# First stage of a two-layer kernel: GpSimd makes both halves of twelve weight splits, two tables move to VectorE

## The reference, cut to what matters

```
# layer 1
c  = x @ W_base^T + b_base + 2 * sum_e w[e] * (x @ As[e]^T) @ Bs[e]^T   # lora with per-row weights
xn = (c - mean) * rsqrt(var + 1e-5) * gamma + beta
s  = max|xn| / 127 ;  q = round(xn / s) ;  wq = alpha * ternary(weight)
x  = x + (q * s) @ wq^T
# layer 2
routing: softmax of 8 logits per row, the best 2 experts, their weights normalised
out = sum over the 2 experts of w * mlp_expert(x) + mlp_shared(x)     # mlp: gelu(x G) * (x U), then D
x = x + quantised_ffn(out)                                            # int16 activations, 4-bit weights
```

## Time and profile before

| | us |
|---|---|
| median of 3 runs (398.55 to 400.49) | 399.46 |
| the profiled execution | 398.53 |
| its span in the profile | 396.8 |
| busy TensorE | 347.6 |
| busy VectorE | 332.6 |
| busy ScalarE | 263.1 |
| busy GpSimd | 231.7 |

### The profile page before, as it was taken

The page is one execution under the profiler, slowest core; times in us unless marked ns, Lnnn a source line. Parts: engine busy times, 40 slices in busy tenths (PEclk is TensorE's granted clock), DMA queues, the critical chain, the costliest instruction groups (busy, mean ns, idle before and its releaser), DMA issues.

```text
span 396.8 us, 6241 instructions
## 1 busy us (share of the span) xinstructions
PE 347.6 (88%) x1759; PEld 286.6 (72%) x1759; DVE 332.6 (84%) x700; ACT 263.1 (66%) x340; POOL 231.7 (58%) x404
## 2 busy tenths in 40 slices
PE   7899987999999999999999999899999972035997
PEld 6677665768898989989898977688577651023797
DVE  4589558976999999999999988876679899989894
ACT  3656687857566665666656545455477899999650
POOL 2647875997466473847465016822095567993552
PEclk9989989999999999999999999999999997555999
DMA  5998994845352443535332005100000000000022
GB/s 165 341 408 295 347 307 133 304 159 213 111 208 108 157 164 113 205 108 186 134 121 91 3 2 170 42 2 0 1 2 1 1 0 0 0 2 1 0 108 106
DMA packets 19850, 47.77 MB, mean 120 GB/s; under 512 B 2787, under 2 KB 8934, under 8 KB 17254
## 3 DMA queue, kind: packets, MB, share of 16 engines
q1 hardware_dynamic: 18342, 47.16, 34.0%
q10 hardware_dynamic: 1472, 0.20, 0.3%
HBM read 33.10 MB, written 12.58 MB: 115 GB/s over the span
## 4 chain that ended last, share of the span: by engine, by line
PE 56%; ACT 12%; DVE 11%; POOL 9%; issue 6%; DMA 4%; POOLq 1%; ACTq 0%; DVEq 0%
PE ps L384 55%; ACT tS L1308 3%; ACT UA L1308 3%; ACT ps L1308 2%; ACT U L1308 2%; DMA wscr<-wst 2%; POOL WD L1547 2%; POOL XCh L1544 2%; DVE unread L1265 2%; DVE O_i L761 2%; DMA bsr<-in_L_cond_Bs_dram 1%; DVE Hl L755 1%; PE ps L381 1%; POOL Hl L1547 1%; POOL wst L1547 1%
## 5 line engine op out<-in xcount | busy, mean ns | idle before, releaser
L1628 POOL CAST xg<-XT 128x64 fp32r x264 | 81.2, 354 | 52.6 <-DVE Hl L755 25.4
L384 PE MATMUL ps<-xg,Wr 128*128 128x384 f32 (+1 forms) x480 | 98.6, 353 | 1.1 <-POOL xg L1628 0.8
L384 PEld LDWEIGHTS ps<-xg,Wr 128*128 128x128 f32 x480 | 85.8, 188 | 8.2 <-POOL xg L1628 1.1
L1308 ACT ACTIVATE Hh<-HbS 128x512 fp32r<-128x512 f32 (+2 forms) x72 | 56.5, 785 | 47.6 <-DVE HbS L755 47.5
L755 DVE TENSOR_TENSOR HbS<-Gb,ps 128x512 f32<-128x512 f32 (+2 forms) x72 | 63.2, 878 | 21.3 <-PE ps L384 18.3
L1308 ACT ACTIVATE Gb<-ps 128x512 f32<-128x512 f32 (+2 forms) x72 | 54.0, 750 | 30.5 <-PE ps L384 28.8
L755 DVE TENSOR_TENSOR Hl<-HbS,Hh 128x768 fp32r<-128x768 f32 (+2 forms) x57 | 59.4, 1042 | 3.5 <-ACT Hh L1308 3.0
L761 DVE SCALAR_TENSOR_TENSOR C<-ps,Wt,C 128x32 f32 x264 | 52.4, 277 | 2.9 <-PE ps L384 2.6
L384 PE MATMUL ps<-XT,SHh 128*128 128x512 f32 x128 | 45.7, 399 | 0.8 <-DVE XT L755 0.4
L1547 POOL TENSOR_TENSOR Hl<-HbS,Hh 128x512 fp32r<-128x512 f32 x15 | 19.5, 1297 | 38.5 <-ACT Hh L1308 38.3
L1308 ACT ACTIVATE ps<-G,S 128x1024 int32<-128x1024 f32 (+2 forms) x30 | 35.8, 1250 | 6.2 <-DVE O_i L761 5.6
(11 more groups left out here) (223 smaller groups left out, 710.8 us busy)
## 6 DMA issues: line engine op xcount, KB each, us to landing
Wr<-wscr SPq DMA_DIRECT2D x20, 1024.0 KB, 4.8
wscr<-wst SPq DMA_DIRECT2D x16, 512.0 KB, 5.9
stg<-n_L_cond_skill_gate_dram SPq DMA_DIRECT2D x8, 256.0 KB, 7.0
stg<-in_L_cond_skill_up_dram SPq DMA_DIRECT2D x8, 256.0 KB, 7.4
wdr<-n_L_cond_skill_down_dram SPq DMA_DIRECT2D x8, 256.0 KB, 5.8
xscr<-X SPq DMA_DIRECT2D x8, 256.0 KB, 6.0
X<-xscr SPq DMA_DIRECT2D x8, 256.0 KB, 4.3
out_dram<-X SPq DMA_DIRECT2D x7, 256.0 KB, 2.0
```

The source lines that it names most:

```text
L384: return e.matmul(o_, l, r, start=start, stop=stop, skip_group_check=True)
L1308: return e.activation(o_, i_, func, **kw)
L1628: last = e.tensor_copy(xg[:, i % XR, :, T * s:T * s + T].rearrange("p a t -> p a t"), XT[:, :, :, bass.ds(regs[s - a_], 1)].rearrange("p a ...
```

## The change

It has six parts.

1. `SPLITS` is now (0, 2, 2, 1, 2, 1, 2, 1, 1, 2, 3, 2). The first `NP` = 12 splits, those of rounds 1 to 8, are made wholly on GpSimd: a copy into the high part (`k_whi`), then the low part. The waits for the load and for the store of the ring's place go with them from ScalarE to GpSimd. The last 7, in rounds 9 to 11, keep their high part on ScalarE.
2. In rounds up to 4, the VectorE instruction on `ST` and the scaled product stand ahead of the second routing block; in rounds 5 and later they keep their place or move a little. In round 5, `hidden(4)` stands ahead of `Pm`.
3. The tables `tmpP` and `iof` (selection of a slot, times its weight) are made on VectorE in round 10 instead of GpSimd in round 9.
4. `down_high` for pieces 0 and 1 stands behind the last table load of ScalarE, and pieces 2 to 7 stand in the loop behind it, at i = 1, 2, 3 (two), 4, 5. Each piece has a semaphore of its own.
5. The rounding waits for the inverse alone (`d_inv`), and column 180 is made by a tensor-scalar instruction.
6. Waits for low parts are spread: `shared_up` waits for 18 of 19, the low part of `XT` for the places of the ring that it overwrites, `shared_down` and GpSimd's clearing of `C` for all 19.

The core of the diff:

```diff
-        SPLITS = (0, 2, 2, 2, 2, 2, 2, 2, 2, 3, 0, 0)
+        SPLITS = (0, 2, 2, 1, 2, 1, 2, 1, 1, 2, 3, 2)
+        NP = sum(SPLITS[:9])
-        WDS = {8: (0,), 10: (1, 2), 11: (3, 4)}
+        WDS = {1: (2,), 2: (3,), 3: (4, 5), 4: (6,), 5: (7,)}
...
     # TensorE
-            w.wait_ge(k_tab, 3)
+            w.wait_ge(d_sel, 2)
             mm(bank[3][:, 0:NSLOT], ones[:, :], tmpP[:, :], True, False)
...
     # VectorE
                     if n == 5:
+                        hidden(4)
+                        w.wait_ge(p_route, 2)
+                        n_ = step(ts(S[:, 44:45], bank[6][:, 16:17], 0.7 / 16384, None, MUL))
                         w.wait_ge(k_const, PART)
                         cp(bcF[:, :], bcI[:, :]).then_inc(d_place, 1)
...
+                i = n - 2
+                if 0 <= i < 8:
+                    w.wait_ge(p_var, i + 1)
+                    if i >= 2:
+                        w.wait_ge(k_rst, i - 1)
+                    ts(ST[:, i % 2, 0:4], AV[:, 0:4], 1.0, 1e-5, MUL, ADD).then_inc(d_var, 1)
+                if n <= 4:
+                    scaled(n - 3)
                 if n == 4:
                     after(n_1, n_2, n_3)
...
+                if n == 10:
+                    ts(tmpP[:, :], iof[:, :], S[:, 42:43], S[:, 38:39], ALU.is_equal, MUL).then_inc(d_sel, 1)
+                    w.wait_ge(d_sel, 1)
+                    ts(iof[:, :], iof[:, :], S[:, 43:44], S[:, 39:40], ALU.is_equal, MUL).then_inc(d_sel, 1)
...
-            step(e.reciprocal(S[:, 183:184], S[:, 182:183]))
+            e.reciprocal(S[:, 183:184], S[:, 182:183]).then_inc(d_inv, 1)
             w.wait_ge(d_rt, n_alpha)
-            tt(S[:, 180:181], S[:, 182:183], S[:, 142:143], MUL).then_inc(d_sc, 1)
+            ts(S[:, 180:181], S[:, 182:183], S[:, 142:143], None, MUL).then_inc(d_sc, 1)
...
     # ScalarE
-                for _ in range(SPLITS[n]):
+                for _ in range(SPLITS[n] if n >= 9 else 0):
...
             do(S[:, 11:12], S[:, 13:14], ACT.Gelu_apprx_tanh)
+            for k in range(2):
+                down_high(k)
             def round_xn(j):
-                w.wait_ge(d_sc, QSC)
+                w.wait_ge(d_inv, 1)
...
     # GpSimd
-                    ts(tmpP[:, :], iof[:, :], S[:, 42:43], S[:, 38:39], ALU.is_equal, MUL).then_inc(k_tab, 1)
-                    ts(iof[:, :], iof[:, :], S[:, 43:44], S[:, 39:40], ALU.is_equal, MUL).then_inc(k_tab, 1)
                 for _ in range(SPLITS[n]):
-                    w.wait_ge(a_whi, split + 1)
+                    if split < NP:
+                        w.wait_ge(s_stg[split % 8], 16 * (split // 8 + 1))
+                        if split >= WRING:
+                            w.wait_ge(s_wst[split % WRING], 16 * (split // WRING))
+                        e.tensor_copy(hi, stg[:, split % 8, :]).then_inc(k_whi, 1)
+                        w.wait_ge(k_whi, split + 1)
+                    else:
+                        w.wait_ge(a_whi, split + 1 - NP)
                     low(lo, stg[:, split % 8, :], hi).then_inc(k_wlo, 1)
```

More of the change, by code:

```diff
@@ L191, in program @@
         s_wst = [sem(f"s_wst{i}") for i in range(WRING)]
+        s_wd = [sem(f"s_wd{i}") for i in range(E)]
         s_wr = [sem(f"s_wr{i}") for i in range(3)]
@@ L207, in program @@
             sem(n) for n in ("d_rt", "d_w2", "d_hot", "d_absw", "d_place", "d_parts", "d_tern", "d_ord", "d_et"))
-        k_tab, d_tab, p_tab = sem("k_tab"), sem("d_tab"), sem("p_tab")
-        k_wlo, k_rst = sem("k_wlo"), sem("k_rst")
-        d_col, p_max, d_top = sem("d_col"), sem("p_max"), sem("d_top")
+        k_tab, d_tab, p_tab, d_sel = sem("k_tab"), sem("d_tab"), sem("p_tab"), sem("d_sel")
+        k_whi, k_wlo, k_rst = sem("k_whi"), sem("k_wlo"), sem("k_rst")
+        d_col, p_max, d_top, d_inv = sem("d_col"), sem("p_max"), sem("d_top"), sem("d_inv")
         d_sc = sem("d_sc")
@@ L523, in shared_up @@
                 w.wait_ge(d_xt, j + 1)
-                w.wait_ge(k_wlo, NR)
+                w.wait_ge(k_wlo, NR - 1)
                 if n >= 2:
@@ L542, in shared_down @@
                 w.wait_ge(a_shh, m + 1)
+                w.wait_ge(k_wlo, NR)
                 if q == 0 and j == 1:
@@ L812, in hidden, with scaled @@
                    w2T[:, :].rearrange("p (a b) -> p a b", a=1).broadcast_to([128, 4, 128]), MUL).then_inc(d_hid, 1)
+            def scaled(i):
+                if 0 <= i < 8:
+                    for h in "ab" if i == 7 else ("",):
+                        w.wait_ge(p_rst, i + 1 + (h == "b"))
+                        w.wait_ge(a_zg, i + 1)
+                        tt(xnT[:, cols(i)][:, SPAN[h]], (A0[1] if h == "b" else AR[i % 2])[:, SPAN[h]], xnT[:, cols(i)][:, SPAN[h]], MUL).then_inc(d_xn, 1)
             for n in range(12):
@@ L916, in _ @@
                         cp(ordI[:, :], bank[6][0:1, 0:NSLOT]).then_inc(d_ord, 1)
-                    hidden(n - 1)
+                    if n > 5:
+                        hidden(n - 1)
                 if n == 9:
@@ L977, in _ @@
                     n_alpha = step(tt(S[:, 142:143], S[:, 141:142], bank[6][:, 19:20], MUL))
[L978 to L988, removed]
-                        tt(xnT[:, cols(i)][:, SPAN[h]], (A0[1] if h == "b" else AR[i % 2])[:, SPAN[h]], xnT[:, cols(i)][:, SPAN[h]], MUL).then_inc(d_xn, 1)
+                if n > 4:
+                    scaled(n - 3)
                 if n == 4:
@@ L1034, in _ @@
                     w.wait_ge(a_xt, i + 1)
+                    if i >= 2:
+                        w.wait_ge(k_wlo, min(NG - 1 + i, NR))
                     low(x_half(1, i), bank[5 + i % 3], x_half(0, i)).then_inc(d_xt, 1)
@@ L1318, in _ @@
             do(S[:, 16:24], S[:, 0:8], ACT.Exp, bias=S[:, 12:13], scale=1.0, accum_out=S[:, 13:14]).then_inc(a_exp, 1)
-            split = 0
+            split = NP
             def down_high(k):
-                w.wait_ge(s_stg[k], 64 if k < 3 else 48)
+                w.wait_ge(s_wd[k], 16)
                 do(WD[:, 0, cols(k)], wdr[:, k, :]).then_inc(a_wdh, 1)
@@ L1363, in _ @@
                     split += 1
-                for k in WDS.get(n, ()):
-                    down_high(k)
             do(S[:, 11:12], S[:, 13:14], ACT.Gelu_apprx_tanh)
+            for k in range(2):
+                down_high(k)
             def shared_gelu(n):
@@ L1397, in _ @@
                     w.wait_ge(p_x1t, i + 1)
-                    w.wait_ge(k_wlo, NR)
                     do(x_half(0, i), bank[5 + i % 3]).then_inc(a_xt, 1)
-                    if 3 <= i < 6:
-                        down_high(2 + i)
+                    for k in WDS.get(i, ()):
+                        down_high(k)
                 n = j - 2
```

8 lines of the change are left out of this document (2 added, 6 removed).

## The result

| | before | after |
|---|---|---|
| median of 8 runs each (us) | 399.78 | 403.49 |
| lowest and highest (us) | 398.55, 402.13 | 401.64, 405.25 |
| ratio, 95% interval | | 1.0091 [1.0069, 1.0114] |
| the profiled execution, its span (us) | 398.53, 396.8 | 401.64, 399.9 |

The changed kernel is slower by 0.9%, about 3.7 us. The forecast was 400.7 with a range up to 402.5: a slowdown, but too small, and the time lies outside the range. I go through the after trace in the order of the prediction. Lines have moved: L386 and L383 are TensorE's helpers, L1324 is ScalarE's, L755 to L767 are VectorE's, L1559, L1562, L1592 and L1604 are GpSimd's. The first rounds of executions end up to 1.2 us apart, so I measure from the variance sum of group 7 (`KC,sq`), "sum 7" in what follows.

The account below looks back on a forecast made before the run. TensorE's rounds 5 to 7, GpSimd's last down_low, then TensorE's experts were taken as the bound. Terms -0.2 - 1.3 + 2.7 + 0.45 - 0.6 + 0.6 = +1.65 on 399.0 gave 400.7 us; range 399.6 to 401.8, with other cases 397.0 to 402.5.

Parts of the forecast that it names:

- Rounds 1 to 4: Without the split on ScalarE, TensorE's variance sum of group 2 and VectorE's hidden(3) come 1.2 us earlier, hidden(3) at best 2.
- the copy's price: GpSimd's high-part copy takes 0.65 us, a split 2.0 to 2.05; the added 8 us cost nothing by themselves.
- the end of both waits: ScalarE's waits of 2.44 us before a split and 2.14 before down_high vanish; round 9's square of group 7 gains 1.3.
- Round 4, the routing block: GpSimd's splits stretch VectorE's block with tables to 5.2 us; followed to round 7, -0.2, from -2.2 free to +0.2 held.
- Tables in round 10: VectorE's two tables wait for GpSimd's low parts ahead of the last scaled product: +2.7 us, ends +0.9 and +3.4.
- ScalarE's tail: From last beta to rounding, high parts, table load, gelu and two down_high take 3.75 us instead of 3.3: +0.45.
- `down_high` in the shared MLP: ScalarE's additional pieces 2 to 4 push Gb, Hh and GpSimd's Hl: +0.6 us, 0.3 to 0.8.
- Rounding and products: Column 180 is off the way and qT of group 1 is freed from GpSimd's low parts: -0.6 us, 0 to -0.9.
- Rival S: TensorE starved about 2 us in round 6 drops to the 0.50 clock where it bounds: +3.3, 402.3 us; chance 0.16.
- The base: Starting time of 399.0 us, put between the profiled 398.53 and the median 399.46, giving 400.7.
- that rule: Whole-instruction port lock makes both VectorE-GpSimd collisions complete: route +0.2, tables +3.1, sum +2.4, 401.4 us.
- the first table's wait: In round 10 VectorE's first table waits 0 to 1.28 us for a GpSimd low part, taken as half, 0.6.

Follow-up runs that it names:

- kernel 1: Changed kernel with both selection tables moved on VectorE from round 10 to round 9, ahead of the variance instruction; 398.92 us, ratio 0.9972.
- kernel 2: Changed kernel with 20 instead of 8 unread filler products on TensorE ahead of the turn of the largest values; 402.13 us, ratio 1.0065.
- kernel 5: kernel 1 plus vneg in GpSimd's round 3, tmpQ in VectorE's round 8, table products ahead of the turn replacing six fillers; 399.95 us, ratio 0.9996.
- kernel 6: Changed kernel with the two selection tables back on GpSimd in round 9; 403.87 us, ratio 1.0096.
- kernel 9: kernel 6 with ScalarE's copy of down piece 1 moved from ahead of the rounding to behind the first XT copy; 402.34 us, ratio 1.0056.
- 10: kernel 5 with 13 unread filling products on TensorE behind the spread of the largest value; 399.85 us, ratio 1.0002.
- Kernel 3: Changed kernel with round 4's variance instruction and scaled product behind the routing block again; 401.90 us, ratio 1.0051.
- 8: kernel 5 with down_high of pieces 2 and 3 moved ahead of ScalarE's first XT copy; 399.63 us, ratio 0.9992.
- kernel 7: kernel 1 with round 4's routing block ahead of the variance instruction and scaled product, as in Kernel 3; 399.31 us, ratio 0.9985.
- 11: 10 with round 4's variance instruction and scaled product behind the routing block again; 399.26 us, ratio 0.999.
- kernel 12: 11 with 8 instead of 2 filling products between the table products and the turn of the largest value; 398.73 us, ratio 0.997.
- 4: Changed kernel with all high parts made on ScalarE, in the same rounds; 403.42 us, ratio 1.0077.

## Why the prediction was wrong, step by step

- **Rounds 1 to 4, the copy's price, the end of both waits**: right (-1.55 of -1.5). But the profile of before itself had the clock at 0.50 in 27 to 28 us, and after had not, so the agreement to 0.05 is partly luck. Sum 7 lies between 48.9 and 50.5 in kernels 1, 2, 5, 6, 9 and 10, which are nearly alike up to there; the latest are 1 and 2, whose profiles have about 3 us at 0.50 ahead of it.
- **Round 4, the routing block**: right in kind and size. With its tables it took 5.5 us (25.02 to 30.50) where I wrote 5.2, and `xTl` came at 30.50 where I wrote 30.7. Kernel 3 shows what it costs: 1.8 us at sum 7 when the clock stays full.
- **Tables in round 10**: right, +2.65 for +2.7; kernel 1 shows it by taking it away (4.17). Before had the clock at 0.50 here too, in 53 to 55 us, which the prediction did not see; beside the 4.17 and 4.18 of kernels 1, 5 and 6 it cost before's 4.35 no more than 0.2.
- **ScalarE's tail**: +0.28 for +0.45. **`down_high` in the shared MLP**: +0.56 for +0.6; the size agrees, but no run isolates the cause, since the one meant to (8) met another wait.
- **Rounding and products** is the step that failed. It reads "`qT` ... -0.6"; measured was +1.00 from rounding to X addition. `qT` was free, but the table products ahead of the first layer-1 product on TensorE took 3.99 us instead of 2.64 at the granted clock of 0.50. My sum carried the delay by the tables, and not what the delay does to the engine that waits for it. Kernels 1, 2 and 3 show this term absent, removed and enlarged. In kernel 2, at the full clock, rounding to X addition is 2.46 (62.37 to 64.83), -0.33 against before and inside the term's own ends of 0 to -0.9. That the clock falls behind such a gap is what the traces show six times of six; kernel 7, where it fell behind one of 1.21, says that the gap is not the only way to it.
- **Rival S** had the mechanism and the wrong place. I looked for TensorE's gap in round 6, where it came (1.49 us at 31.82) and the clock stayed at 1.00, and not behind round 10, where my own +2.7 opened one of 3.66 us. S's number, 402.3, rests on the wrong place too.
- **The base.** I added the sum to 399.0; the median of before over 8 runs is 399.78, which is 0.78 of the error. The profiles' difference is 3.11 where I had 1.65, another 1.46, of which 1.35 is the table products. The last 0.60 is that after's median lies 1.85 above its profiled execution and before's 1.25. These add up to the 2.8 us by which I was short.

By the Trainium skill ("SBUF — State Buffer", Who interferes with whom) the shared port is held for the whole instruction. By that rule I had given 401.4. The prediction puts the whole distance to its own sum down to the first table's wait; that is 0.4 of the 0.8, and the other 0.4 is the routing block (-0.2 against +0.2). For the big operands this case agrees (tables of 1.52 and 1.35 beside low parts of 1.28). The smallest were not all held, as the last section shows; the rule counts a tensor-scalar only in its two-port mode, and no row tells whether those ran in it.

What stays open: kernels 5, 7, 8, 10, 11 and 12 each remove a shown wait, and only 12 and 1 come out below before by more than their intervals. Their traces differ in where the clock fell more than in their order of work, and one profile for each can't say how often it falls where.

## What to carry over

A delay that is added ahead of a wait of TensorE must be priced twice: once for the wait and once for the instructions behind the wait at the 0.50 clock, so list what stands in TensorE's order behind each gap that the change opens or lengthens. A short VectorE instruction with SBUF operands belongs where GpSimd is itself waiting (kernel 1: 0.68 and 0.53 us) and not beside its chain of long ones (1.52 and 1.35). When work is moved from one engine to another, look at what its old place fed: here low parts fed loads, loads fed a copy, and the copy stood ahead of the rounding (kernel 6); low parts also fed stores, and the first `Gb` waits for these (kernel 9). And when an edit has several parts, read the waits of the stretch that each part touches: the early `vneg` of kernel 5 went into four more kernels before its half microsecond was seen.

## What the runs showed of the hardware

- **The time of a single execution goes with its mean granted clock.** Each run lists it, and with it much of the spread within one kernel is explained (mean us, runs in brackets; "before" is its 93 runs of the three sessions but one, which took 402.9 at 0.936):

| mean clock | before | after | kernel 1 | kernel 12 |
|---|---|---|---|---|
| 0.940, 0.941 | 401.8 (9) | 404.2 (2) | | |
| 0.944, 0.945 | 401.1 (14) | 403.6 (5) | | 401.3 (1) |
| 0.948, 0.949 | 399.6 (57) | | 399.4 (4) | 400.6 (3) |
| 0.953 | 398.8 (12) | 401.6 (1) | 399.3 (4) | 398.5 (4) |
| 0.957 | | | 398.2 (4) | 397.3 (4) |

  In one row after is 2.4 to 2.8 us slower than before; the rest of the 3.7 goes with its runs lying at lower clocks (mean 0.945, before 0.948). The rows are wide, though: in the third, before's 21 runs at 0.948 average 398.8 and its 36 at 0.949 average 400.1, so this split is an estimate. Kernels 1 and 12 are in some rows above before and in some below it: what they gain is that 8 of their 12 runs each lie at 0.953 and 0.957, and 12 of before's 93. A gain in such a kernel can be a shift between rows of this table.
- **The same gap does not always lower the clock.** At 30 to 32 us TensorE was idle for 1.93 and 1.95 us in kernels 5 and 10, which are the same program up to there; the clock was 0.50 in 34 to 36 us in the one and 1.00 in the other. Ahead of the turn, kernels 1 and 7 waited 1.23 and 1.21 us; the table products behind ran at 1.00 in the one and at 0.50 in the other. After gaps of 3.64 to 4.76 us (after and kernels 3, 4, 5, 6, 8) it was at 0.50 each time, at the latest 1.7 us behind the return of work (58.30 and 60.0 after), and in kernel 5 already ahead of it (0.52 in 60 to 61, work from 61.06).
- **The smallest instructions are not all held.** `S<-S` of 128x1 as a tensor-scalar took 0.19 us beside a low part (59.85 to 61.5 us on GpSimd); as a tensor-tensor it took 0.96, to the end of the low part. And `tmpP` was not held by GpSimd's power of 128x4 (0.46 beside 1.01). The first of these rows:

```profile
60.59 0.19 DVE L761 TENSOR_SCALAR S<-S 128x1 f32<-128x1 f32 x1
```
